# Node passes as later stages of the edge-attention loop, with one wait per chunk on GpSimd's gathers

## The chip, the cores and the metric

The kernel runs on one core of one Trainium2 chip. The metric is the device time of one execution in microseconds (us). Before the change it is 2722.23 us, the median of 3 runs (2716.83 to 2722.79).

## The reference, cut to what matters

A graph of 6250 nodes (128 features) and 100000 edges, sorted by their target `dst`. First comes a graph transformer layer, then a message layer; each is added to its input and normalised.

```python
q, k, v = x @ Wq, x @ Wk, x @ Wv                        # 8 heads of 16
scores = einsum('ehd,ehd->eh', q[dst], k[src]) / sqrt(16)
ex = exp(scores - segment_max(scores, dst)[dst])
alpha = ex / (segment_sum(ex, dst)[dst] + 1e-9)
agg = segment_sum(alpha[:, :, None] * v[src], dst)
h1 = layer_norm(x + agg @ W0, ln1_g, ln1_b)
ff = relu(h1 @ fc1_w + fc1_b) @ fc2_w + fc2_b           # 512 hidden
x1 = _layernorm(x + layer_norm(h1 + ff, ln2_g, ln2_b))
# message layer: for each half of the edges, over [x1[src], edge_attr, req]
m = relu(cat @ W1 + b1) @ W2 + b2
h = (1 + eps) * x1 + segment_sum(m_forward, dst) + segment_sum(m_backward, dst)
out = _layernorm(x1 + relu(h @ Wu + bu))
```

## The kernel before, in words

**Stages.** A start forms the table `kvq_tab` (keys, values, queries of all nodes) and the tables of chunks. Then come an edge loop, the node passes, and a message loop.

**Edge loop.** The edges are cut into 56 chunks of 1792 (128 lanes of 14), each with a window of 128 nodes. GpSimd gathers keys and values of a chunk with 14 indirect DMAs (L670, `gather_chunk`) into one of RING = 4 slots; a chunk has four pieces of 4, 3, 4 and 3 gathers (PIECES). A chunk passes through stages on the other engines: `passes4` runs one body for the chunk `new`, with `a_`, `b_`, `c_`, `e_` the chunks one to four before it.

- `new`: TensorE spreads the window's queries over the edges with one-hot matrices (L1078, `queries`, one PSUM bank a piece; it posts `l_q`). VectorE multiplies them by the keys and sums per head (L1445, L1447, `scores`), then takes running maxima (L1456, L1457; it posts `l_ml`).
- `a_`: two transposes (L1092, L1093, post `l_lr`), scans across the lanes (L1463 to L1465, `across`), two transposes back (L1112, L1113, post `l_cd`).
- `b_`: VectorE forms the differences to the maximum (L1472 to L1477), ScalarE the exponentials (L848 to L850), VectorE one-hot masks (L1494) and the weighted values (L1499, two halves, post `l_pva` and `l_pvb`). TensorE sums them over the window in 14 products (L1102, posts `l_agg`).
- `c_`: ScalarE copies the sums (L839), VectorE divides and adds what is carried between windows (L1485 to L1490, `averages`), TensorE transposes (L1118) and carries (L1119, post `l_ra`).
- `e_`: ScalarE copies the transposed averages into `nodes`, which holds all nodes (L843).

ScalarE also forms the one-hot matrices of a chunk two ahead (L811, L815, L816, `lane_masks`), from two lines of lane positions that VectorE subtracts (L1436, L1437, `lanes`) and ScalarE scales (L809).

What sets the order is the code itself: each engine has its body with waits in it, and nothing is reordered. A gather's slot is free when `l_pvb` of four chunks before is posted; beyond that, piece 1 of a chunk waits for `l_agg`, piece 2 for `l_q` and piece 3 for `l_lr`, all posted by TensorE.

**Node passes** (`passes3`, ten groups of five tiles of 125 nodes): W0, first normalisation, fc1, relu, fc2, second and third normalisation, the product `y` with the upper part of W1, stored to `y_tab`. ScalarE takes square roots (L871), normalises (L880) and copies; GpSimd adds and multiplies rows (L693 to L704), and clears the accumulators of the message loop (L700, L701).

**Message loop.** It gathers rows of `y_tab` (L727), adds the edge attributes (TensorE L1239, VectorE L1635), applies relu (ScalarE L957), sums over the window (L1252), accumulates (L1626, L1628), and normalises and stores a finished window. ScalarE's L976 and L979, and VectorE's L1649, stand in that last part. The gathers wait for the products of four chunks before (`m_agg`), a post of TensorE.

## Time and profile before

| | before |
|---|---|
| time, median of 3 runs | 2722.23 us |
| the profiled execution | 2717.23 us |
| its span, first to last instruction | 2715.2 us |
| busy: TensorE (PE) | 1557.6 us, 57% |
| TensorE weight loads (PEld) | 1227.2 us, 45% |
| VectorE (DVE) | 1442.3 us, 53% |
| ScalarE (ACT) | 748.1 us, 28% |
| GpSimd (POOL) | 1592.9 us, 59% |
| mean granted TensorE clock | 0.719 |
| moved by DMA | 251.96 MB, 93 GB/s |

Busy time counts neither waits nor the issuing of a DMA that goes through a queue; GpSimd's indirect gathers are instructions of their own and do count. A share is an average over stages with different limits. In the chain that ended last, 29% of the span is "issue", time in which the engine waited for nothing that the profile shows, 25% TensorE, 19% "another core or an unknown queue" (in rows: "remote"), 15% VectorE.

### The profile page before, as it was taken

How to read it: one execution, taken by the hardware profiler on the slowest of the kernel's cores; microseconds unless marked ns; L12 is line 12 of the kernel's file. 1: busy time of each engine (PE TensorE's matmuls, PEld its weight loads, DVE VectorE, ACT ScalarE, POOL GpSimd, SP SyncE). 2: the span in 40 equal slices, each digit the busy share in tenths (PEclk: the TensorE clock that was granted, in tenths of full speed). 3: DMA queues.
4: the chain of work that ended last, by engine and by line, in shares of the span. 5: the costliest groups of instructions: out<-in, count | busy, mean ns of one | idle time of the engine just before them, and what ended most of it. 6: DMA issues, size and time to landing. Idle time of an engine off the chain costs nothing.

```text
span 2715.2 us, 32144 instructions
## 1 busy us (share of the span) xinstructions
PE 1557.6 (57%) x7355; PEld 1227.2 (45%) x7356; DVE 1442.3 (53%) x2972; ACT 748.1 (28%) x1512; POOL 1592.9 (59%) x1662
## 2 busy tenths in 40 slices
PE   6354565556555555556786354556465565654656
PEld 4244455545545554455664233344343443433434
DVE  5265666666666666666575134345254353443535
ACT  3333333333433333333574011111111111111111
POOL 3665666666666666662532756665656656656661
PEclk9567767767777676767898566677677776767767
DMA  7554444444444444442011211221211212211221
GB/s 250 146 172 140 141 135 133 132 145 133 133 129 146 133 133 129 146 133 76 18 42 44 54 47 51 51 57 49 54 50 50 58 51 52 55 51 50 54 54 28
DMA packets 148256, 251.96 MB, mean 93 GB/s; under 512 B 74681, under 2 KB 99401, under 8 KB 147179
## 3 DMA queue, kind: packets, MB, share of 16 engines
q0 software_dynamic: 64048, 156.29, 20.2%
q1 hardware_dynamic: 83612, 94.45, 11.3%
q10 hardware_dynamic: 560, 0.82, 0.1%
q8 instruction: 13, 0.21, 0.0%
q14 instruction: 23, 0.19, 0.0%
HBM read 229.88 MB, written 21.54 MB: 93 GB/s over the span
## 4 chain that ended last, share of the span: by engine, by line
issue 29%; PE 25%; another core or an unknown queue 19%; DVE 15%; DVEq 5%; ACT 3%; DMA 2%; POOL 0%; SPq 0%; ACTq 0%; PEldq 0%; POOLq 0%
PE ps L1102 10%; PE ps L1078 8%; DVE arena L1626 4%; DVE arena L1635 2%; DVEq L1655 2%; DVE arena L1499 1%; ACT arena L880 1%; DVEq L1654 1%; PE ps L1029 1%; DMA arena<-d 1%; PE ps L1119 1%; DVEq L1652 1%; DVE arena L1445 1%; DVE arena L1554 1%
## 5 line engine op out<-in xcount | busy, mean ns | idle before, releaser
L670 POOL DMA_INDIRECT arena<-kvq_tab,arena x784 | 748.1, 954 | 455.7 <-issue 249.2
L727 POOL DMA_INDIRECT arena<-y_tab,arena x784 | 742.6, 947 | 447.5 <-issue 229.1
L1252 PEld LDWEIGHTS ps<-arena 128*128 128x128 f32 x1568 | 294.5, 255 | 407.5 <-issue 376.6
L1252 PE MATMUL ps<-arena 128*128 128x128 f32 x1568 | 319.1, 346 | 268.4 <-issue 250.9
L1102 PE MATMUL ps<-arena 128*128 128x136 f32 x1568 | 322.0, 393 | 245.7 <-issue 132.3
L1102 PEld LDWEIGHTS ps<-arena 128*128 128x128 f32 x1568 | 312.4, 297 | 268.2 <-issue 268.2
L957 ACT ACTIVATE arena<-arena 128x512 f32<-128x512 f32 x224 | 119.4, 569 | 800.1 <-DVE arena L1635 504.8
L1078 PE MATMUL ps<-arena 128*128 128x128 f32 x1596 | 286.7, 350 | 72.1 <-issue 32.3
L1239 PE MATMUL ps<-w1blk,eaT 113*128 x456 | 284.9, 709 | 64.8 <-issue 64.2
L1078 PEld LDWEIGHTS ps<-arena 128*128 128x128 f32 x1596 | 265.9, 258 | 98.4 <-issue 98.4
L1445 DVE TENSOR_TENSOR arena<-ps,arena 128x512 f32<-128x512 f32 x224 | 136.9, 611 | 320.8 <-remote 316.0
L1635 DVE TENSOR_TENSOR arena<-ps,arena 128x512 f32<-128x512 f32 x224 | 128.4, 618 | 318.0 <-remote 256.2
L816 ACT ACTIVATE arena<-arena 128x1792 f32<-128x1792 f32 x58 | 189.7, 3271 | 0.0
L1628 DVE TENSOR_REDUCE arena<-arena 128x128 f32<-128x1792 f32 x57 | 182.2, 3196 | 2.0
L1447 DVE TENSOR_REDUCE arena<-arena 128x32 f32<-128x512 f32 x224 | 139.2, 622 | 7.7
L1239 PEld LDWEIGHTS ps<-w1blk,eaT 113*128 113x128 f32 x456 | 95.2, 252 | 80.0 <-issue 80.0
L1494 DVE TENSOR_TENSOR arena<-ps,arena 128x1792 f32<-128x1792 f32 x56 | 113.3, 2024 | 26.9 <-issue 14.7
L1649 DVE BATCH_NORM_STATS2 arena<-ps 128x6 f32<-128x128 f32 x56 | 16.4, 292 | 202.2 <-remote 155.2
L826 ACT ACTIVATE arena<-arena 128x15 f32<-128x15 f32 x57 | 12.4, 217 | 384.5 <-issue 282.1
L1499 DVE TENSOR_TENSOR arena<-arena,ps 128x896 f32<-128x896 f32 x112 | 116.2, 1079 | 0.0
L1626 DVE TENSOR_TENSOR arena<-ps,arena 128x1792 f32<-128x1792 f32 x57 | 114.3, 2005 | 0.0
L1661 DVE TENSOR_TENSOR arena<-arena,ps 128x128 f32 x56 | 16.2, 289 | 171.9 <-issue 140.6
(258 smaller groups left out, 1973.1 us busy)
## 6 DMA issues: line engine op xcount, KB each, us to landing
arena<-d SPq DMA_DIRECT2D x59, 897.0 KB
arena<-kvq_tab,arena POOLq DMA_INDIRECT x784
arena<-y_tab,arena POOLq DMA_INDIRECT x784
kvq_tab<-arena SPq DMA_DIRECT2D x7, 1344.0 KB, 7.0
arena<-in_edge_attr_dram SPq DMA_DIRECT2D x60, 112.0 KB
y_tab<-arena SPq DMA_DIRECT2D x10, 625.0 KB
arena<-kvq_tab SPq DMA_DIRECT2D x59, 64.0 KB
out_dram<-arena SPq DMA_DIRECT2D x56, 64.0 KB
```

What stands on the lines that cost most here:

```text
L670: g.indirect_dma_start(kv_s[:, r, t, :], None, kvq_tab.rearrange("n (a d) -> (n a) d", a=3), bass.IndirectOffsetOnAxis(ap=v3(idx, RING)[:, ...
L727: g.indirect_dma_start(yg_s[:, r, t, :], None, y_tab, bass.IndirectOffsetOnAxis(ap=v3(idx1, RING)[:, r, t:t + 1], axis=0)).then_inc(m_g[r] ...
L816: a.activation(hotT.rearrange("n (u g e) -> n u g e", u=2, g=G)[:, u, :, :], line.rearrange("n (e g) -> n g e", g=G), ACT.Relu, scale=-1.0 ...
L1078: last = mm(bank(k)[:, t * D:(t + 1) * D], hotT_s[:, u, s0 + t, :], v3(qwin, 2)[:, u, :])
L1102: last = mm(sums, hot_s[:, u, t, :], contrib_s[:, u, t * RW:(t + 1) * RW], start=(t == 0), stop=(t == G - 1))
L1239: mm(bank(j)[:, 0:n * D], eaT_s[:, u, k * P:(k + 1) * P], w1blk[:, ds(way + a0 * D, n * D)]).then_inc(m_u, 1)
L1252: last = mm(bank(6 + u)[:, 0:W], yg_s[:, r, t, :], hot1_s[:, u, t, :], start=(t == 0), stop=(t == G - 1))
L1445: tt(keys, v3(bank(k)[:, 0:n * D], n), keys, ALU.mult).then_inc(l_prod, 1)
L1499: tt(contrib_s[:, u, s0:s1, :, 0:DH], kv_s[:, r, s0:s1, D:2 * D].rearrange("p g (h w) -> p g h w", h=H), weights.rearrange("p (g h) -> p g ...
L1626: link(tt(hot1_s[:, u, :, :], columns1[:, None, :].to_broadcast([P, G, W]), dcr1[:, :, None].to_broadcast([P, G, W]), ALU.is_equal))
L1628: v.tensor_reduce(v3(hsum, 2)[:, u, :], hot1_s[:, u, :, :].rearrange("p g n -> p n g"), AX_X, ALU.add).then_inc(m_hot, 1)
L1635: tt(rows_, v3(bank(j)[:, 0:n * D], n), rows_, ALU.add).then_inc(m_hid, 1)
```

## The change

The node passes go as a stage of their own. Their work is done for each chunk's window of 128 nodes, as four later stages of the edge loop (`passes8`, with LEAD = 8 passes ahead of the loop and 8 behind it):

- `e_`: ScalarE copies the transposed averages to `aggT` instead of `nodes`; TensorE multiplies by W0 and adds the window's features with a placement matrix (`sh`, `xw`), which SyncE loads from x and from the new table `moves` (`load_features`).
- `f_`: moments and first normalisation.
- `g_`: transpose, fc1, relu, fc2, and with them the scaled transpose and the features again for the sum.
- `h_`: moments, second normalisation with the sum, moments, third.
- `k_`: transpose, copy into `nodes`, `y`, and SyncE's store to `y_tab` (`store_y`).

The root's inverse is now `Exp(-0.5 * Ln(v + eps))` on ScalarE (`unit`) in place of a square root and a reciprocal. `lanes` goes from VectorE; two small products on TensorE from `dd` (two activations) give the same lines. The queries use two PSUM banks, not four: pieces 2 and 3 of a chunk are computed in its own pass, pieces 0 and 1 of the next chunk at the end of the pass. GpSimd keeps the waits for the index load and for `l_pvb`. Clearing the accumulators moves to VectorE, ahead of the message loop. SyncE's first loads for the message loop move into the passes that empty the pipeline.

The core of the diff:

```diff
-ITERS0 = -(-(NB0 + N // W - RING) // RING)
+LEAD = 2 * RING
+ITERS0 = -(-(NB0 + N // W - LEAD) // RING)
+        def passes8(eng, one_pass, n):
+            for c in range(LEAD):
+                one_pass(c % RING, *(c - k if c >= k else None for k in range(9)))
+            with eng.Fori(0, n) as i:
+                for c in range(RING):
+                    one_pass(c, *(i * RING + (c + LEAD - k) for k in range(9)))
+            for c in range(8):
+                one_pass(c % RING, *(n * RING + (c + LEAD - k) if k > c else None for k in range(9)))
...
+            def load_features(chunk, r):
+                base = entry0(chunk, 2, N - W)
+                sp.dma_start(v3(xw, RING)[:, r, :], x[ds(base, W), :]).then_inc(l_xw[r], 16)
+                lower = entry0(chunk, 3, W)
+                sp.dma_start(v3(sh, RING)[:, r, :], moves[ds(lower, P), :]).then_inc(l_xw[r], 16)
...
             def gather_chunk(r):
                 pool.wait_ge(l_ix[r], landed)
                 pool.wait_ge(l_pvb, slot_free)
                 for k, (s0, n) in enumerate(PIECES):
-                    if k:
-                        pool.wait_ge(s_init, 3)
-                    if k == 1:
-                        pool.wait_ge(l_agg, slot_free)
-                    if k == 2:
-                        pool.wait_ge(l_q, asked)
-                    if k == 3:
-                        pool.wait_ge(l_lr, turned_)
...
+            def unit(at):
+                link(a.activation(lnv[at], mv[at][:, 1:2], ACT.Ln, bias=eps_ln[:, :]))
+                return a.activation(rstd[at], lnv[at], ACT.Exp, scale=-0.5)
+            def normalised(to, rows_, at):
+                link(unit(at))
+                link(a.activation(shift[at], neg[at], ACT.Identity, scale=rstd[at]))
+                return a.activation(to, rows_, ACT.Identity, scale=rstd[at], bias=shift[at])
...
+                if h_ is not None:
+                    act.wait_ge(n_v2, minus7)
+                    unit(1).then_inc(n_s2, 1)
...
+                if g_ is not None:
+                    act.wait_ge(n_fcp, minus6)
+                    for c in range(FC):
+                        last = a.activation(v3(ffT, FC)[:, c, :], bank(2)[:, c * W:(c + 1) * W], ACT.Relu, bias=fc1b_all[:, c:c + 1])
+                    last.then_inc(n_f1s, 1)
...
+                if g_ is not None:
+                    pe.wait_ge(n_n1, minus6)
+                    last = tp(bank(3)[:, 0:W], h1n, ident[:, :])
+                if k_ is not None:
+                    pe.wait_ge(n_x1, minus8)
+                    last = tp(bank(3)[:, W:2 * W], x1, ident[:, :])
+                if new is not None:
+                    queries(u, 2, True)
+                if e_ is not None:
+                    pe.wait_ge(l_avT, minus4)
+                    mm(seven[:, W:2 * W], aggT, w0_sb[:, :], start=True, stop=False)
+                    last = mm(seven[:, W:2 * W], v3(sh, RING)[:, r, :], v3(xw, RING)[:, r, :], start=False, stop=True)
...
+                    pe.wait_ge(n_f1s, minus6)
+                    for c in range(FC):
+                        mm(six[:, 2 * W:3 * W], v3(ffT, FC)[:, c, :], fc2_sb[:, c, :], start=(c == 0), stop=False)
+                    last = mm(six[:, 2 * W:3 * W], h1Tr, ident[:, :], start=False, stop=True)
+                if a_ is not None or c_ is not None or g_ is not None:
+                    last.then_inc(l_cd, 1)
...
                 if new is not None:
                     scores(r, 0)
                 if b_ is not None:
                     differences((r + 2) % RING)
+                if f_ is not None:
+                    dve.wait_ge(n_res, minus1)
+                    link(moments(0, v3(res, 2)[:, 1 - u, :]))
+                    ts(neg[0], mv[0][:, 0:1], -1.0, None, ALU.mult).then_inc(n_v1, 1)
                 if new is not None:
                     scores(r, 1)
+                if h_ is not None:
+                    dve.wait_ge(l_cd, minus2)
+                    moments(1, bank(6)[:, 2 * W:3 * W]).then_inc(n_v2, 1)
+                    stt(tq, bank(6)[:, 2 * W:3 * W], mv[1][:, 0:1], g2_rows[:, :], ALU.subtract, ALU.mult).then_inc(n_tq, 1)
+                if new is not None:
+                    steps(1 - u, (r + 1) % RING)
                 if b_ is not None:
                     masks(u)
                     weighted(u, (r + 2) % RING)
+                if h_ is not None:
+                    stt(s3, tq, rstd[1], bank(6)[:, 3 * W:4 * W], ALU.mult, ALU.add).then_inc(n_s3, 1)
+                    link(moments(2, s3))
```

**GpSimd in the edge loop.** The first block is one chunk before the change, and the second two chunks of the changed kernel (L682 is the gather, formerly L670).

```order
L670 DMA arena<-kvq_tab,arena 128x256 [waits l_pvb,l_ix0,s_init]
L670 DMA arena<-kvq_tab,arena 128x256 x3
L670 DMA arena<-kvq_tab,arena 128x256 [waits l_agg,s_init]
L670 DMA arena<-kvq_tab,arena 128x256 x2
L670 DMA arena<-kvq_tab,arena 128x256 [waits l_q,s_init]
L670 DMA arena<-kvq_tab,arena 128x256 x3
L670 DMA arena<-kvq_tab,arena 128x256 [waits l_lr,s_init]
L670 DMA arena<-kvq_tab,arena 128x256 x2
L672 ISA
```

```order
L682 DMA arena<-kvq_tab,arena 128x256 [waits l_pvb,l_ix0,s_init]
L682 DMA arena<-kvq_tab,arena 128x256 x13
L684 REGISTER_ALU
L682 DMA arena<-kvq_tab,arena 128x256 [waits l_pvb,l_ix1,s_init]
L682 DMA arena<-kvq_tab,arena 128x256 x13
L684 REGISTER_ALU
```

The three waits inside a chunk's gathers are gone, and the fourteen follow one another.

**ScalarE in a pass of the edge loop.** Before, this is the stretch from the copy of the sums to the lane lines. After, the stretch from the exponentials to the product `y`; L827 is the Ln and L828 the Exp of `unit`, L887 the copy of the embedding, L894 the relus, L899 the copy of `y`.

```order
L839 ACTIVATE arena<-ps 128x136 [waits l_agg]
L841 ISA
L841 TENSOR_LOAD tab_sb
L841 ISA x2
L843 ISA [waits l_ra]
L843 ACTIVATE nodes<-ps 128x128
L848 ACTIVATE ps<-arena 128x112 [waits l_d,l_lr]
L849 ACTIVATE arena<-arena 128x112
L850 ACTIVATE arena<-arena 1x8
L826 ACTIVATE arena<-arena 128x15 [waits l_dif]
L827 ACTIVATE arena<-arena 128x8x13
L829 REGISTER_ALU
```

```order
L878 ACTIVATE ps<-arena 128x112 [waits l_d,l_lr]
L879 ACTIVATE arena<-arena 128x112
L880 ACTIVATE arena<-arena 1x8
L827 ACT_TABLE_LOAD
L827 ACTIVATE xs<-xs,eps_ln 128x1 [waits n_v2]
L828 ACT_TABLE_LOAD
L828 ACTIVATE xs<-xs 128x1 [waits n_al]
L887 ACTIVATE xs<-ps 128x128 [waits n_emb]
L889 ACTIVATE arena<-ps 8x256
L894 ACTIVATE xs<-ps,fc1b_all 128x128 [waits n_fcp]
L894 ACTIVATE xs<-ps,fc1b_all 128x128 x3
L899 ACTIVATE xs<-ps 128x256 [waits n_yfree,n_yp]
```

The exponentials are now followed by a normalisation's Ln and Exp, each with a table load of its own; the same pair of loads comes before each of the other two normalisations of a pass, so six loads a chunk. The lane masks come later, after the copies of the embedding, the relus and the copy of `y`.

## Rows read from the trace of the kernel before

Engines in the rows: PE is TensorE, PEld its weight loads, DVE VectorE, ACT ScalarE, POOL GpSimd. A stretch's row has its start and end, its length, the busy us (and count of instructions) of PE, PEld, DVE, ACT and POOL, TensorE's granted clock, the share of the DMA engines' time and GB/s. A group's row has line, engine, operation, output and input and their shapes and the count, then busy us and mean ns of one, then the idle us just before them and what ended most of it. A timeline's row has start and length in us, and in brackets the idle time before it and what ended that.

**Rows 1.** Busy time of each engine in the three stages.

```profile
67.00:1244.00 1177.00, 650.67 (x3390) 583.67 (x3391) 742.07 (x1613) 414.67 (x705) 747.85 (x784) 0.70 0.46 139
...
1295.00:1491.00 196.00, 148.50 (x852) 116.54 (x852) 125.17 (x442) 118.12 (x222) 75.33 (x42) 0.90 0.10 34
1491.00:2715.00 1224.00, 682.97 (x2758) 470.84 (x2758) 506.61 (x731) 174.75 (x509) 742.72 (x785) 0.69 0.20 51
```

**Rows 2.** Groups by line, whole span.

```profile
L670 POOL DMA_INDIRECT arena<-kvq_tab,arena x784 | 748.1, 954 | 455.7 <-issue 249.2 <-remote 188.4 <-PE ps L1078 15.7
...
L1445 DVE TENSOR_TENSOR arena<-ps,arena 128x512 f32<-128x512 f32 x224 | 136.9, 611 | 320.8 <-remote 316.0 <-PE ps L1078 4.9
...
L839 ACT ACTIVATE arena<-ps 128x136 f32<-128x136 f32 x56 | 15.9, 284 | 188.3 <-remote 171.7 <-PE ps L1102 16.6
```

**Rows 3.** Timeline of POOL in the edge loop.

```profile
703.93 0.96 POOL L670 DMA_INDIRECT arena<-kvq_tab,arena  x1 [0.30 <-issue]
708.46 0.95 POOL L670 DMA_INDIRECT arena<-kvq_tab,arena  x1 [3.57 <-remote]
...
729.40 0.94 POOL L670 DMA_INDIRECT arena<-kvq_tab,arena  x1 [2.93 <-remote]
```

**Rows 4.** Timeline of PE in the edge loop.

```profile
728.52 2.92 PE L1078 MATMUL ps<-arena 128*128 128x128 f32 x12 [0.36 <-issue]
...
745.84 0.27 PE L1118 MATMUL ps<-ident,arena 128*128 128x128 f32 x1 [2.23 <-issue]
748.66 0.39 PE L1119 MATMUL ps<-arena 128*1 128x136 f32 x1 [2.56 <-issue]
```

**Rows 5.** Timeline of ACT in the edge loop.

```profile
749.57 0.29 ACT L839 ACTIVATE arena<-ps 128x136 f32<-128x136 f32 x1 [3.92 <-remote]
```

**Rows 6.** Timeline of DVE in the edge loop.

```profile
728.81 0.69 DVE L1445 TENSOR_TENSOR arena<-ps,arena 128x512 f32<-128x512 f32 x1 [6.14 <-remote]
...
734.81 2.08 DVE L1499 TENSOR_TENSOR arena<-arena,ps 128x896 f32<-128x896 f32 x2
```

**Rows 7.** Message loop: one stretch of its start, and timelines of DVE and POOL.

```profile
1531.00:1557.00 26.00, 4.84 (x9) 2.59 (x9) 0.56 (x1) 0.81 (x3) 19.73 (x21) 0.50 0.20 53
...
1557.96 0.69 DVE L1635 TENSOR_TENSOR arena<-ps,arena 128x512 f32<-128x512 f32 x1 [26.04 <-remote]
...
1559.96 0.94 POOL L727 DMA_INDIRECT arena<-y_tab,arena  x1 [0.30 <-issue]
...
2030.56 0.69 DVE L1635 TENSOR_TENSOR arena<-ps,arena 128x512 f32<-128x512 f32 x1 [3.68 <-remote]
```

**Rows 8.** Timeline of ACT after the last gather, and in the node passes.

```profile
1235.32 0.36 ACT L848 ACTIVATE ps<-arena 128x112 f32<-128x112 f32 x1 [3.05 <-PE ps L1093]
...
1249.82 0.36 ACT L848 ACTIVATE ps<-arena 128x112 f32<-128x112 f32 x1 [0.55 <-DVE arena L1477]
...
1288.63 0.20 ACT L864 ACTIVATE mark<-eps_ln 128x1 f32<-128x1 f32 x1
...
1296.06 1.28 ACT L871 ACT_TABLE_LOAD   x1
1297.36 0.30 ACT L871 ACTIVATE arena<-arena,eps_ln 128x5 f32<-128x5 f32 x1
```

**Rows 9.** One stretch of the edge loop, and groups by line.

```profile
800.00:1000.00 200.00, 114.41 (x611) 103.59 (x611) 130.05 (x288) 73.64 (x125) 127.93 (x134) 0.72 0.43 134
...
L880 ACT ACTIVATE arena<-arena 128x128 f32<-128x128 f32 x100 | 40.7, 484 | 9.3 <-DVE arena L1561 9.3
...
L976 ACT ACTIVATE arena<-ps,bucol 128x128 f32<-128x128 f32 x56 | 20.0, 358 | 4.8 <-PE ps L1273 4.8
...
L1649 DVE BATCH_NORM_STATS2 arena<-ps 128x6 f32<-128x128 f32 x56 | 16.4, 292 | 202.2 <-remote 155.2 <-issue 44.2 <-PE ps L1273 2.8
...
L979 ACT ACTIVATE arena<-arena,eps_ln 128x1 f32<-128x1 f32 x56 | 16.3, 290 | 2.6 <-DVE arena L1650 2.6
...
L700 POOL MEMSET arena<- 128x12756 f32 x1 | 10.7, 10731 | 0.0
```

More of the change, by code:

```diff
@@ L110, in gnn_kernel @@
         i1 = dram("i1", (ALL1,), I32)
+        moves = dram("moves", (2 * P, W), F32)
         tab1 = dram("tab1", (TE, TF), I32)
@@ new lines, in sp_edges @@
+            def sp_edges(r, new, a_, b_, c_, e_, f_, g_, h_, k_):
+                u = r % 2
+                if new is not None:
+                    if b_ is not None:
+                        sp.wait_ge(s_d0, 48)
+                        sp.wait_ge(l_dcr, picked)
+                    load_heads(new + 2, (r + 2) % RING)
+                    sp.wait_ge(s_arr, 16 * 3)
+                    sp.wait_ge(l_q, asked)
+                    load_queries(new + 2, u)
+                    sp.wait_ge(s_d0, 48)
+                    sp.wait_ge(l_hT, formed)
+                    load_line(new + 3)
+                    sp.wait_ge(s_arr, 16 * 3)
+                    sp.wait_ge(l_ml, ended)
+                    load_index(new + 4, r)
+                if new is None and a_ is not None:
+                    sp.wait_ge(s_tabi, 48)
+                    for c in range(RING):
+                        load_chunk(c, c)
+                if b_ is not None:
+                    sp.wait_ge(s_tab0, 3)
+                    sp.wait_ge(s_move, 32)
+                    if g_ is not None:
+                        sp.wait_ge(l_cd, seen)
+                    load_features(b_, (r + 2) % RING)
+                if k_ is not None:
+                    store_y(k_, u)
+                for c in (ended, picked, formed, seen, turned8):
@@ L1031, in _ @@
                     turn_table()
+            pe.wait_ge(s_tab0, 2)
+            for f in range(2):
+                last = tp(bank(7)[0:1, (f + 1) * TE:(f + 2) * TE], tbe[0:TE, f + 2:f + 3], ident[0:TE, 0:TE])
+            last.then_inc(s_turn, 1)
             pe.wait_ge(s_ca, acts(PT - 1))
@@ L1083, in queries, with pe_edges @@
                         pe.reg_add(window, window, 16)
-            def pe_edges(r, new, a_, b_, c_, e_):
+            def pe_edges(r, new, a_, b_, c_, e_, f_, g_, h_, k_):
                 u = r % 2
                 w = 1 - u
-                left_right, sums, carried, turned = bank(4), bank(5)[:, 0:RW], bank(6), bank(7)
+                left_right, sums, six, seven = bank(4), bank(5)[:, 0:RW], bank(6), bank(7)
+                if type(new) is int and new == 4:
+                    pe.wait_ge(s_wn, 16 * 9)
+                    pe.wait_ge(s_tab0, 3)
+                    for c in range(FC):
+                        last = mm(bank(2)[:, c:c + 1], fc1_sb[:, c * P:(c + 1) * P], ln1_cols[:, 1:2])
+                    last.then_inc(n_b1, 1)
+                if type(new) is int and new == 6:
+                    pe.wait_ge(n_fc1, 2)
+                    pe.wait_ge(n_b1s, FC)
+                if type(new) is int and new == 7:
+                    pe.wait_ge(s_w4, 16 * LATE)
                 if a_ is not None:
@@ L1120, in pe_edges @@
-                if new is not None:
-                    queries(w, 2, True)
-                    queries(w, 3, True)
-                for c in (minus1, minus2, minus3, minus4):
+                for c in (now, minus1, minus2, minus3, minus4, minus6, minus7, minus8, minus9):
                     pe.reg_add(c, c, 1)
-            for k in range(NP_):
+            for k in range(2):
                 queries(0, k, False)
-            passes4(pe, pe_edges, n0, 4)
+            passes8(pe, pe_edges, n0)
@@ L1196, in turn_rows @@
-            def turn_rows(new, old, out_):
-                if out_ is not None:
-                    pe.wait_ge(n_ys, out_ + 2)
-                if new is not None:
-                    pe.wait_ge(n_res, new + 1)
-                pe.wait_ge(n_x1, old + 1)
-                transposes(bank(0, 2), res2, n_xTp)
-            for c in range(FC):
-                last = mm(bank(4)[:, c:c + 1], fc1_sb[:, c * P:(c + 1) * P], ln1_cols[:, 1:2])
-            last.then_inc(n_b1, 1)
-            pe.sem_inc(n_xTp, 1)
@@ L1519, in dve_edges @@
                     averages(1 - u, (r + 1) % RING, c_)
-                if new is not None:
-                    steps(1 - u, (r + 1) % RING)
-                    lanes((r + 2) % RING)
                 if new is not None:
```

625 lines of the change are left out of this document (260 added, 365 removed).

## The prediction

> **What bounds the kernel now.** I read the table of stretches first, to see which stages the time is in. The three rows [rows 1] are the first edge loop, the node passes and the message loop. Both loops issue 784 gathers on GpSimd (POOL); 1177 us / 56 chunks = 21.0 us a chunk in the first. The node passes are 196 us in which TensorE works 148.5 and GpSimd 75.3, and no gather runs.
>
> Next, who sets those 21 us. The groups by line [rows 2] say that a gather takes 954 ns, and that VectorE and ScalarE lose most of their idle time to "remote": 316 us before the score products L1445, 172 us before the copy L839. The timeline of GpSimd [rows 3] shows the rhythm: a gather each 0.95 + 0.30 = 1.255 us, 14 in a row 17.3 us with one short stop, and once a chunk a gap of 3.57 or 2.93 us ended by "remote". What stands still outside that gap is TensorE. Its two last transposes and carry products start at 745.84 and 748.66, 2.2 and 2.6 us apart with no producer named [rows 4], although the gathers run without a break there. The copy L839, which needs nothing but the 14 aggregation products, starts at 749.57 after 3.92 us of "remote" [rows 5], and L1445 of the chunk before, with its queries long computed, starts at 728.81 after 6.14 us [rows 6], 0.6 us before the gap at 729.40 ends. I read this as: **while GpSimd issues gathers without a break, TensorE's completions (and much of its issue) hardly get through; they come in a burst 2 to 3 us after the last gather.** (The gap of 2.93 less those 0.6 is 2.3, the gap of 3.57 less 0.6 is 3.0 [rows 3]; I take 2.8.) VectorE then needs 728.81 to 736.8 = 8.0 us to the end of the weighted values L1499 [rows 6].
>
> The message loop tests that reading. At its start 56 gathers run unpaused; in 26 us of them TensorE starts 9 matmuls, VectorE one instruction, and VectorE waits 26.04 us in one piece [rows 7]. Against it: a product at 2030.56 came through in the middle of a run after 3.68 us [rows 7]. So the hold leaks somewhat.
>
> Without gathers ScalarE's L848 goes from 1235.32 to 1249.82 [rows 8]: a pass costs 14.5 us, so the gathers cost 6.4 us of each chunk.
>
> **What the change does to GpSimd.** Now a slot's fourteen gathers wait for their index load and for `l_pvb` of four chunks before, and nothing else. Before, pieces 1, 2 and 3 also waited for `l_agg`, `l_q` and `l_lr`, all posted by TensorE, so that GpSimd could not run far ahead of it. With the ring of four full, the next gathers start when VectorE posts L1499 of a chunk and run 14 x 1.255 = 17.6 us to the start of the next, 17.3 to the end of the last. Everything VectorE then needs from TensorE (queries of pieces 2 and 3, `l_cd`) is posted after those weighted values are read, so inside the hold. The cycle closes on itself: 0.5 us to resume + 17.3 of gathers + 2.8 to the burst + the chain to the next L1499. That chain was 8.0 us [rows 6] with the queries of the whole chunk ready. Now there stand in it the moments of the embedding (three instructions) and those of the feed-forward with a scaling (three), each about 0.3 by the nearest row, L1649's 292 ns [rows 9], so 1.9 us, and the steps, 0.2; with one more link between engines I take 10.3. **T = 0.5 + 17.3 + 2.8 + 10.3 = 30.9 us a chunk, against 21.0.** Bounds of T: 25, if as much leaks as at 2030.56 and the burst comes before the gathers end; 34, if pieces 2 and 3 of the scores, whose queries are now only half a chunk ahead, fall into the next burst.
>
> **What it does to ScalarE.** It has 73.64 us of work in 200 [rows 9], 7.7 a chunk. It gains, per chunk: six table loads (each Ln and each Exp of the three normalisations has its own), at 1.28 each [rows 8] 7.7; ten instructions on one column or one number at L979's 0.29, 2.9; two normalisations and the scaled copy at L880's 0.484, 1.45; eight copies and relus of 128x128 at L976's 0.358 and the wider y copy at 0.484 [rows 9], 3.35. Together 15.4, so 23.1 us a chunk, packed. That is below T = 30.9: covered. It is above today's 21.0, so without the hold ScalarE would be the bound.
> The row shows the table load's 1.28 us and the next instruction at 1297.36, 0.02 us after it [rows 8]. The Trainium skill ("ScalarE: Activation LUTs", What ACT_TABLE_LOAD costs) adds a drain and comes to 2.66 us a switch; by that ScalarE would be at 23.1 + 6 x 1.38 = 31.4 us a chunk, just above T. The row shows no such drain, and it decides. The same page (Table sets: the hidden batching unit) has one set with both Ln and Exp, which would need one load for all; the build has six, so I count six.
>
> **TensorE, VectorE, SyncE.** TensorE goes from 36 to 52 matrix products a chunk; let go, it runs 12 instructions in 2.92 us [rows 4], so the some 20 products between burst and weighted values, two instructions each, take about 10: its own time just hides behind VectorE's chain of 10.3, if no answer of ScalarE's stands between; if one does, that is the upper end. VectorE loses the two lane instructions and gains about 3.5 us, of which 2.1 lie in the chain. SyncE adds a load of 128 KB and a store of 128 KB a chunk, and past them only its next loads are queued, two passes ahead: nothing; the DMA engines are busy 0.46 of the first loop [rows 1]. The clearing of the accumulators, 10.7 us and more on GpSimd [rows 9], moves to VectorE at the start of the message loop, where it waits for 26 us at one place [rows 7]: hidden; if not, +11 and somewhat more.
>
> **Sum.** Before, the message loop starts at 1491. After: the first 56 gathers run unpaused from 67 to 138, the burst is at 141, and the first weighted values, behind two passes and a half of scores, at 160. Fifty-one more at 30.9, less 7 for the first ones, whose passes lack the node stages: 1729. Gathers and burst once more: 1750, L1499 of the 53rd chunk 1760. Then no gathers are left and ScalarE's packed work sets the pace: 25 us to the next L1499, 15 to the end of the last full pass, and eight passes that empty the pipeline, an estimated 17.9 for the first two, which form no new lane masks, down to 4 for the last, together 108: 1908, and 5 to the last store and barrier: 1913. That is **+422**. Put the other way: before, the edge loop and its tail end at 1289 [rows 8] and 202 us of node passes and barriers follow; these go, and the loop with its tail grows by 624. The message loop keeps its waits: 1224. The profiled execution took 2717.2 (span 2715.2), 5.0 under the median 2722.2, within what its runs differ. 2717.2 + 422 = 3139; I say 3140. Each us of T is 51 us of time, and T = 30.9 - 422 / 51 = 22.6 would break even.
>
> **Rivals.**
> *Partial leak* (T 25 to 28): for it the product at 2030.56. At T = 26, 3140 - 51 x 4.9 = 2890. 0.16.
> *A longer chain* (T over 34, or ScalarE's loads dearer): pieces 2 and 3 in the next burst, or Ln waiting on VectorE and back within the burst. At T = 34, 3300; with the skill's drain T = 33, about 3250. The part over 3310 has 0.06.
> *The other side: TensorE's completions are not held on this path, and ScalarE is the bound.* Then the waits taken out cost nothing, the node passes vanish under the loop, and the time is decided by ScalarE's packing: from the 141 of the start, 141 + 56 x 23.1 = 1435 against 1491, so -56: 2661. It wins up to (1491 - 141) / 56 = 24.1 us a chunk; with 1.7 us of waits a chunk between its own links it would be at 2756. For it: the 196 us that go are real, and the gap that ends a hold may be a wait for the very semaphores that are removed, so that the pause was the cause of nothing. Against it: the message loop, where 26 us pass with no such wait. 0.12.
> *The change doesn't do what it says*: the table loads could be skipped when executed; ScalarE is then at 15.4 a chunk, and under the hold nothing changes: 3140 still.
>
> **How the numbers follow.** The hold with T from 28 to 34: 0.63, its own range 2990 to 3300. Leak 0.16, longer or dearer 0.06, ScalarE-bound and faster 0.12, about equal 0.03. 0.2% (5 us) is what a measurement of this kernel can tell from none. Faster 0.12, same 0.03, slower 0.85. The range leaves out those two and the part over 3310: 2780 to 3310.
>
> **What would show it.** Right: gathers of the first loop in blocks of 14 with one gap of 11 to 16 us, none inside; VectorE's and ScalarE's "remote" waits above 12 us a chunk; the first loop 1.4 times as long; TensorE's clock lower there. ScalarE busy near 23 us a chunk with six loads of 1.28, and not waited for. Wrong: gaps on GpSimd under 7 us, or ScalarE busy over 90% of a pass; then the hold was not there and the loads set the time. If L1499 comes much over 11 us after the burst, the chain term was too small.

## The result, and the profile after

| | before | after |
|---|---|---|
| time, median | 2719.53 us (4 runs, 2716.22 to 2722.79) | 3085.15 us (4 runs, 3078.35 to 3091.03) |
| ratio to before | | 1.134, 95% interval 1.131 to 1.137 |
| span of the profiled execution | 2715.2 us | 3082.6 us |
| busy: TensorE | 1557.6 us | 1594.0 us |
| VectorE | 1442.3 us | 1419.3 us |
| ScalarE | 748.1 us | 1360.3 us |
| GpSimd | 1592.9 us | 1514.5 us |

The change makes the kernel 13% slower; forecast were 3140 us, 2780 to 3310. A run over 1.5% longer than the fastest of the same kernel is slow and is compared with nothing; that was one run, in experiment 5. Busy time hardly grows except on ScalarE, and ScalarE is busy only 44% of the span. The stages show where the time went; these are stretches of the changed kernel, with the columns of [rows 1]:

```profile
67.00:1719.00 1652.00, 783.26 (x5017) 659.89 (x5017) 802.18 (x1975) 1036.62 (x2052) 743.85 (x784) 0.76 0.34 105
1719.00:1860.00 141.00, 85.19 (x440) 69.00 (x441) 62.20 (x179) 126.78 (x261) 0.00 (x0) 0.71 0.11 34
1860.00:3083.00 1223.00, 678.48 (x2758) 470.08 (x2757) 521.32 (x732) 175.09 (x508) 742.68 (x785) 0.70 0.20 51
...
600.00:1000.00 400.00, 197.36 (x1287) 165.82 (x1287) 203.44 (x509) 269.71 (x539) 172.59 (x182) 0.78 0.33 101
```

The edge loop up to its last gather takes 1652 us where it took 1177, the emptying of the pipeline 141 where tail and node passes took 247 (1244 to 1491), and the message loop 1223 where it took 1224: +475, -106, -1. In the 400 us from 600 on ScalarE is busy 269.7, two thirds, and each other engine about half of the time or less. Nothing is full, so the loop is bound by waits.

The groups by line of the changed kernel (L682 is the gather, L1422 the score products, L869 the copy of the transposed rows, the first in ScalarE's pass that needs a later product than the aggregation and the transposed averages), as in [rows 2]:

```profile
L682 POOL DMA_INDIRECT arena<-kvq_tab,arena x784 | 743.8, 949 | 930.2 <-DVE arena L1476 674.3 <-issue 255.9
...
L1422 DVE TENSOR_TENSOR arena<-ps,arena 128x512 f32<-128x512 f32 x224 | 138.7, 619 | 789.0 <-remote 764.8 <-issue 13.8 <-PE ps L1081 10.4
...
L869 ACT ACTIVATE xs<-ps 128x128 f32<-128x128 f32 x56 | 15.5, 277 | 369.3 <-remote 367.4 <-PE ps L1115 1.5 <-issue 0.2
```

GpSimd waits 674 us for VectorE's L1476, the weighted values (L1499 before); VectorE waits 765 us for "remote" before L1422, and ScalarE 367 before L869. That is a circle. The timelines show one turn of it; first GpSimd, against [rows 3]:

```profile
912.40 0.95 POOL L682 DMA_INDIRECT arena<-kvq_tab,arena  x1 [13.49 <-DVE arena L1476]
...
928.70 0.95 POOL L682 DMA_INDIRECT arena<-kvq_tab,arena  x1 [0.30 <-issue]
943.10 0.95 POOL L682 DMA_INDIRECT arena<-kvq_tab,arena  x1 [13.46 <-DVE arena L1476]
```

Fourteen gathers run from 912.40 to 929.65, then nothing for 13.46 us. The turns are 30.7 us long. TensorE and VectorE in the same turn:

```profile
910.75 3.48 PE L1153 MATMUL ps<-arena 128*128 128x136 f32 x28 [1.95 <-DVE arena L1476]
...
915.66 0.33 PE L1170 MATMUL ps<-identw,arena 128*128 128x128 f32 x1
...
916.56 1.16 PE L1176 MATMUL ps<-fc_sb,xs 128*128 128x128 f32 x8
...
917.78 1.73 PE L1081 MATMUL ps<-arena 128*128 128x128 f32 x14
...
924.22 0.47 PE L1115 MATMUL ps<-identw,xs 128*128 128x128 f32 x1 [4.39 <-ACT xs L834]
...
901.87 0.69 DVE L1422 TENSOR_TENSOR arena<-ps,arena 128x512 f32<-128x512 f32 x1 [14.34 <-remote]
...
909.53 2.08 DVE L1476 TENSOR_TENSOR arena<-arena,ps 128x896 f32<-128x896 f32 x2
...
932.57 0.69 DVE L1422 TENSOR_TENSOR arena<-ps,arena 128x512 f32<-128x512 f32 x1 [14.31 <-remote]
```

TensorE has finished the aggregation at 914.2, the transposed averages (L1170) at 916.0, fc2 (L1176) and, by 919.5, the queries (L1081) that VectorE's next L1422 needs; its records there are dense. VectorE starts it at 932.57, 13 us later and 2.9 us after the last gather has ended. Nothing but the report of that work (the semaphore post) is missing. The trace's semaphore events, which no view prints, have it directly: the posts for the second batch of products (carries and fc2, both pieces of the queries, the maxima's transposes, the transpose of 924.22) stand at 932.38 to 932.64, while those products end from 917.94 to 924.69. The other thing that L1422 needs, the landing of its gathers, stands at 888.12. ScalarE:

```profile
905.85 1.28 ACT L827 ACT_TABLE_LOAD   x1
907.25 0.29 ACT L827 ACTIVATE xs<-xs,eps_ln 128x1 f32<-128x1 f32 x1
...
924.57 0.26 ACT L851 ACTIVATE arena<-ps 128x136 f32<-128x136 f32 x1
924.73 0.27 ACT L854 ACTIVATE xs<-ps 128x128 f32<-128x128 f32 x1
...
932.66 0.28 ACT L869 ACTIVATE xs<-ps 128x128 f32<-128x128 f32 x1 [7.30 <-remote]
```

The two copies that need the aggregation (L851) and the transposed averages (L854) start at 924.57 and 924.73, without a wait, as soon as ScalarE comes to them: what TensorE finished up to 916.0, 3.6 us into the run of gathers, had been reported (the post for L1170 stands at 916.70). What it finished later had not: L869, which needs the transpose of 924.22, waits till 932.66 as VectorE does. Of the six loads of tables (1.28 us each, and their instruction 0.1 us behind) four lie in the stretch in which VectorE works, and two, at 920.21 and 921.81, ahead of the transpose of 924.22, whose report is held anyway. Whether they cost something is tested in experiment 2.

### The profile page after: what moved, and what is told of

Same layout as the page of the kernel before. It is cut to its first block, busy times and chain, and to the rows that moved or that the text cites. A ratio compares the mean times of both kernels' runs of the same rounds, so it can differ in the third digit from the quotient of the medians.

```text
span 3082.6 us, 37672 instructions
## 1 busy us (share of the span) xinstructions
PE 1594.0 (52%) x8385; PEld 1228.9 (40%) x8386; DVE 1419.3 (46%) x2981; ACT 1360.3 (44%) x2857; POOL 1514.5 (49%) x1622
## 3 DMA queue, kind: packets, MB, share of 16 engines
q1 hardware_dynamic: 105794, 99.14, 10.3%
## 4 chain that ended last, share of the span: by engine, by line
another core or an unknown queue 35%; issue 23%; DVE 22%; ACT 7%; PE 7%; DVEq 4%; DMA 1%; SPq 1%; ACTq 0%; POOLq 0%
DVE arena L1422 4%; DVE arena L1476 3%; DVE arena L1560 3%; PE ps L1218 2%; ACT L828 2%; PE ps L1231 2%; DVE arena L1569 2%; ACT L827 1%; DVEq L1589 1%; DVE arena L1471 1%; DVE xs L1481 1%; PE ps L1021 1%; DVEq L1588 1%; DVE arena L1424 1%
## 5 line engine op out<-in xcount | busy, mean ns | idle before, releaser
L682 POOL DMA_INDIRECT arena<-kvq_tab,arena x784 | 743.8, 949 | 930.2 <-DVE arena L1476 674.3
L711 POOL DMA_INDIRECT arena<-y_tab,xs x784 | 742.6, 947 | 573.4 <-issue 371.5
L1081 PE MATMUL ps<-arena 128*128 128x128 f32 x1582 | 268.4, 328 | 482.0 <-DVE arena L1422 423.6
L1422 DVE TENSOR_TENSOR arena<-ps,arena 128x512 f32<-128x512 f32 x224 | 138.7, 619 | 789.0 <-remote 764.8
L1231 PE MATMUL ps<-arena 128*128 128x128 f32 x1568 | 314.6, 343 | 282.9 <-issue 273.9
L1231 PEld LDWEIGHTS ps<-arena 128*128 128x128 f32 x1568 | 291.3, 253 | 415.3 <-issue 394.5
L1081 PEld LDWEIGHTS ps<-arena 128*128 128x128 f32 x1582 | 243.5, 237 | 499.1 <-issue 498.9
L1153 PE MATMUL ps<-arena 128*128 128x136 f32 x1568 | 205.6, 291 | 96.9 <-DVE arena L1476 96.9
L1153 PEld LDWEIGHTS ps<-arena 128*128 128x128 f32 x1568 | 196.1, 199 | 117.7 <-issue 117.6
L828 ACT ACT_TABLE_LOAD x168 | 215.5, 1283 | 3.0
L827 ACT ACT_TABLE_LOAD x168 | 215.5, 1283 | 3.0
L869 ACT ACTIVATE xs<-ps 128x128 f32<-128x128 f32 x56 | 15.5, 277 | 369.3 <-remote 367.4
L1115 PE MATMUL ps<-identw,xs 128*128 128x128 f32 x56 | 26.3, 470 | 242.1 <-ACT xs L834 220.2
L944 ACT ACTIVATE eaT<-ps 112x256 f32<-112x256 f32 x59 | 21.7, 367 | 258.9 <-remote 238.1
L1471 DVE TENSOR_TENSOR arena<-ps,arena 128x1792 f32<-128x1792 f32 x56 | 113.0, 2018 | 14.7 <-ACT arena L880 14.7
```

The costliest lines, as they stand in the source:

```text
L682: g.indirect_dma_start(kv_s[:, r, t, :], None, kvq_tab.rearrange("n (a d) -> (n a) d", a=3), bass.IndirectOffsetOnAxis(ap=v3(idx, RING)[:, ...
L711: g.indirect_dma_start(yg_s[:, r, t, :], None, y_tab, bass.IndirectOffsetOnAxis(ap=v3(idx1, RING)[:, r, t:t + 1], axis=0)).then_inc(m_g[r] ...
L827: link(a.activation(lnv[at], mv[at][:, 1:2], ACT.Ln, bias=eps_ln[:, :]))
L828: return a.activation(rstd[at], lnv[at], ACT.Exp, scale=-0.5)
L1081: last = mm(bank(k % 2)[:, t * D:(t + 1) * D], hotT_s[:, u, s0 + t, :], v3(qwin, 2)[:, u, :])
L1153: last = mm(sums, hot_s[:, u, t, :], contrib_s[:, u, t * RW:(t + 1) * RW], start=(t == 0), stop=(t == G - 1))
```

## The experiments

**Theory (hold):** while GpSimd issues gathers without a break, TensorE's completions stay back; the three waits of before made the breaks. **Rivals:** ScalarE's table loads made it slow; or the longer chain of stages did, whatever GpSimd does. All ratios below are to runs of the kernel before on the same chip, which took 2715.64 to 2729.84 us (medians). All of the chunk times are from the gathers of chunks 15 to 45 of each trace's edge loop, from the first of one to the first of the other, divided by 30; by this measure before has 20.9 us and the change 30.3.

### 1. The three waits back in the changed kernel

```diff
                 for k, (s0, n) in enumerate(PIECES):
+                    if k == 1:
+                        pool.wait_ge(s_init, 3)
+                        pool.wait_ge(l_agg, slot_free)
+                    if k == 2:
+                        pool.wait_ge(s_init, 3)
+                        pool.wait_ge(l_q, asked)
+                    if k == 3:
+                        pool.wait_ge(s_init, 3)
+                        pool.wait_ge(l_lr, turned_)
```

`asked` starts at BASE - 2 and grows by 4 a chunk: the first half of the queries of the chunk after `new`. `turned_` starts at BASE - 1 and grows by 1. The lines that make and raise these counters are left out, here and below. `s_init` is complete before the loop (its last post stands at 69.85 us in the changed kernel) and holds nothing up.

> The changed kernel with the three waits of before put back inside a chunk's gathers: piece 1 for the aggregation four chunks back, piece 2 for the queries of the next chunk's first half, piece 3 for the transposes of the pass after. Hold theory (TensorE's completions stay back while gathers run on, and come 2.8 us after the last): the pause lets them out once in the middle, so a chunk falls from 30.7 us to what ScalarE's 23.1 us of work plus some waits allow, 24 to 25; 3085 - 51 x 6.2 = about 2770 (2720 to 2850). Rival (the pauses are without effect, and the chain through four stages more is simply longer): 3085 or, with the pauses' 3 us a chunk on top, up to 3230.

Measured: 2738.1 us (2722.7 to 2750.4, 10 runs), ratio 1.002 (0.9995 to 1.005). 23.6 us a chunk. With the waits the whole loss of 13% is gone: with all four new stages, six table loads a chunk and the queries half a chunk ahead, it is even with before. One stretch, and GpSimd's gaps:

```profile
600.00:1000.00 400.00, 268.60 (x1639) 230.89 (x1639) 262.15 (x646) 346.55 (x699) 226.77 (x238) 0.79 0.42 132
...
814.10 0.95 POOL L693 DMA_INDIRECT arena<-kvq_tab,arena  x1 [3.23 <-DVE arena L1489]
...
820.68 0.95 POOL L693 DMA_INDIRECT arena<-kvq_tab,arena  x1 [1.87 <-remote]
...
836.20 0.96 POOL L693 DMA_INDIRECT arena<-kvq_tab,arena  x1 [3.27 <-DVE arena L1489]
```

Several shorter gaps (1.9 to 3.3 us here, up to 7.0 elsewhere in the loop), mostly after 4, 7 or 10 gathers, take the place of one of 13.5. ScalarE is busy 346.6 of 400; experiment 3 tests whether it is now the bound.

### 2. One table load in place of six a chunk

```diff
+            a.add_instruction(mybir.InstLoadActFuncSet(name=nc.get_next_instruction_name(), act_func_set_id=6,
+                engine=mybir.EngineType.Activation, ins=[], outs=[]))
             penalties(0, 0)
```

The loop uses Ln, Exp, Identity, Copy, Relu and Square; with set 6 loaded by hand ahead of it, the trace has no other table load between 70 and 1959 us.

> The changed kernel with one table set that holds Ln and Exp loaded once, so without the six table loads a chunk (7.7 us of ScalarE). Hold theory: ScalarE is not what a chunk waits for (30.7 us are gathers, burst and VectorE's chain), so the edge loop keeps 30.6 to 30.7 us a chunk; only the tail after the last gather, eight passes at ScalarE's pace, gets shorter by up to 8 x 5 = 40 us: 3045 to 3085. Rival (ScalarE's loads are what made the change slow): 56 x 7.7 = 430 less, about 2655.

Measured: 3062.8 us (3053.8 to 3068.6), ratio 1.121 (1.119 to 1.124). ScalarE's busy time and the tail, from the last gather (start at 1731.6) to the message loop's first (1836.2):

```profile
600.00:1000.00 400.00, 197.46 (x1271) 170.24 (x1272) 202.13 (x503) 167.20 (x459) 172.57 (x182) 0.74 0.33 101
...
1732.00:1836.00 104.00, 72.34 (x440) 61.57 (x441) 61.98 (x179) 62.08 (x211) 0.56 (x1) 0.83 0.16 48
```

ScalarE falls from 269.7 to 167.2 us of 400, from 20.4 to 12.8 us a chunk, and the chunk has 30.6 us where it had 30.3. The tail is 104.6 us in place of 143.2 (starts at 1716.9 and 1860.1); of these 38.6 us the loop, 15 us longer, takes some back. The medians differ by 22 us; by the ratios to before (1.134 and 1.121, on two chips) it is 35. The loads were covered in the loop. The rival of the loads falls.

### 3. Both together

> Both edits: the three waits and one table load. Hold theory: with the pause and without the loads ScalarE has 15.4 us a chunk, the gathers with one gap (17.3 + 3.5) bound again: 21 us a chunk, 3085 - 51 x 9.7 - 40 in the tail = about 2550 (2530 to 2620), faster than before, since the 196 us of node passes are really gone. Rival (loads alone): 2655 as with one load only. Rival (longer chain alone): 3045 to 3085.

Measured: 2758.6 us (2752.7 to 2767.2), ratio 1.011 (1.008 to 1.014), 25.0 us a chunk: a miss by 200 us, and slower than with the loads. The gaps are irregular, and what ends them is another:

```profile
802.17 0.95 POOL L693 DMA_INDIRECT arena<-kvq_tab,arena  x1 [4.83 <-PE ps L1167]
...
809.98 0.95 POOL L693 DMA_INDIRECT arena<-kvq_tab,arena  x1 [4.34 <-PE ps L1095]
812.03 0.95 POOL L693 DMA_INDIRECT arena<-kvq_tab,arena  x1 [1.11 <-issue]
...
827.42 0.95 POOL L693 DMA_INDIRECT arena<-kvq_tab,arena  x1 [3.14 <-remote]
...
L693 POOL DMA_INDIRECT arena<-kvq_tab,arena x784 | 746.4, 952 | 650.2 <-issue 258.3 <-PE ps L1167 206.6 <-PE ps L1095 156.1
```

Four gaps in 30 us, of 1.1 to 4.8 us, and a run of ten gathers between the last two. GpSimd waits 206.6 us in all for L1167, the aggregation, and 156.1 for L1095, the queries, with TensorE named: there TensorE's work itself was late, not only its report. The products of L1167 show it:

```profile
790.98 3.01 PE L1167 MATMUL ps<-arena 128*128 128x136 f32 x16 [3.08 <-DVE arena L1490]
...
798.47 0.39 PE L1167 MATMUL ps<-arena 128*128 128x136 f32 x1 [1.74 <-issue]
799.20 2.20 PE L1167 MATMUL ps<-arena 128*128 128x136 f32 x9 [0.35 <-issue]
```

The gathers of that stretch run to 797.34. Under them TensorE starts single products 0.9 to 1.7 us apart, and the last nine follow in a row 1.9 us after the gathers' end. Over the loop these 28 products take 10.0 us in the median chunk; in the changed kernel and in experiment 1 it is 3.5. So gathers hold back TensorE's issue too when they fall on such work. ScalarE was not what bound experiment 1, since its busy time fell without any gain. Why the kernel without the loads comes to lie so badly is not shown; 7 and 8 show which wait mends it.

### 4. The kernel before without its three waits

```diff
-                    if k:
-                        pool.wait_ge(s_init, 3)
-                    if k == 1:
-                        pool.wait_ge(l_agg, slot_free)
-                    if k == 2:
-                        pool.wait_ge(l_q, asked)
-                    if k == 3:
-                        pool.wait_ge(l_lr, turned_)
```

> The kernel before with the three waits inside a chunk's gathers taken out, nothing else: one wait per chunk as in the change. Hold theory: 0.5 + 17.3 + 2.8 + 8.0 = 28.6 us a chunk in place of 20.9: +7.7 x 51 = +390, about 3110 (3000 to 3150). Rival (the waits are a cost or nothing): 2719 or less.

Measured: 3072.1 us (3065.6 to 3078.8), ratio 1.125 (1.123 to 1.128), 27.5 us a chunk. No stage moved, no table load, no longer chain: taking out the three waits alone costs nearly as much as the whole change (1.134). GpSimd's first gather of two chunks (L662), and VectorE's score products, differences and weighted values (L1437, L1464, L1491):

```profile
811.36 0.95 POOL L662 DMA_INDIRECT arena<-kvq_tab,arena  x1 [0.30 <-issue]
822.63 0.95 POOL L662 DMA_INDIRECT arena<-kvq_tab,arena  x1 [10.32 <-DVE arena L1491]
...
850.24 0.95 POOL L662 DMA_INDIRECT arena<-kvq_tab,arena  x1 [10.33 <-DVE arena L1491]
...
810.82 0.69 DVE L1437 TENSOR_TENSOR arena<-ps,arena 128x512 f32<-128x512 f32 x1 [10.23 <-remote]
...
815.05 0.23 DVE L1464 SCALAR_TENSOR_TENSOR arena<-ps,arena 128x8 f32<-128x8 f32 x1 [2.82 <-remote]
...
819.73 2.08 DVE L1491 TENSOR_TENSOR arena<-arena,ps 128x896 f32<-128x896 f32 x2
```

The gathers end at 812.3 and VectorE's queries were reported 1.5 us before that, at 810.8; but the carries for L1464 only at 815.05, 2.7 us behind. The 1.1 us that are missing to the expected 28.6 are such a leak. The rival of the longer chain falls too.

### 5. A stop on GpSimd that waits for nobody

```diff
                 for k, (s0, n) in enumerate(PIECES):
+                    if k == 2:
+                        pool.wait_ge(m_gap, gap_)
+                        pool.reg_add(gap_, gap_, 1)
+                        g.tensor_tensor(idle_.rearrange("p (b c) -> p b c", b=11), ones[:, None, :].to_broadcast([P, 11, P]),
+                                        ones[:, None, :].to_broadcast([P, 11, P]), ALU.add).then_inc(m_gap, 1)
```

`idle_` is an unused tile of 128x1408 and `ones` the constant, repeated; `m_gap` is posted by the addition itself, one chunk before.

> The changed kernel, no wait on another engine added: after seven of a chunk's fourteen gathers GpSimd does one addition of 128x1408 constants into an unused tile, some 3.4 us by the 1.55 us of a 128x640 one in the kernel before. Hold theory (what keeps TensorE's completions back is the unbroken issue of gathers): the stop is long enough for the burst, 2.8 us after the seventh, VectorE's chain of 10 us runs under the second seven, and a chunk falls from 30.7 to 23.5 to 26 us: 2720 to 2850. Rival (only waiting for TensorE helps, because it orders the two engines): nothing gained, 3.4 us a chunk more, 3085 to 3280.

Measured: 2813.8 us, one run (the other took 2889.0), 1.035 of before; 25.0 us a chunk. One run gives no interval, but it is 271 us less than the change, and even the other is 196 less, far outside of what runs of one kernel differ by here. GpSimd, and VectorE's L1430 (the score products):

```profile
825.19 0.95 POOL L690 DMA_INDIRECT arena<-kvq_tab,arena  x1 [0.30 <-issue]
826.16 2.54 POOL L687 TENSOR_TENSOR xs<-ones 128x1408 f32<-128x1408 f32 x1
828.86 0.95 POOL L690 DMA_INDIRECT arena<-kvq_tab,arena  x1 [0.16 <-issue]
...
828.17 0.69 DVE L1430 TENSOR_TENSOR arena<-ps,arena 128x512 f32<-128x512 f32 x1 [4.22 <-remote]
```

The seventh gather ends at 826.14, GpSimd adds for 2.54 us, and 2.0 us into this VectorE's wait ends, at 828.17. GpSimd was not idle and waited for nobody. The posts stand at 827.84 to 828.20 in the semaphore events. What lets the completions out is the break in the gathers.

### 6. One wait only

After seven gathers, for `l_q` and `asked` as in 1.

> The changed kernel with a single wait put back: after seven gathers, for the queries of the next chunk's first half. It lets out the carries, these queries and the transposes behind them. Hold theory: one burst in the middle and one before the run gives nearly what three waits gave: 2740 to 2800. If each of the three waits is needed, 2850 or more.

Measured: 2888.2 us (2883.2 to 2893.1), ratio 1.062 (1.056 to 1.069), 26.8 us a chunk. So one place gives 200 us of the 350, not nearly all; the expectation of 2740 to 2800 was wrong, and its other case came.

### 7. Which posts have to come out

A pass needs TensorE's posts in two batches: carries, transposes and the next chunk's first half of queries; then, after ScalarE's answer to the transposes, embedding, fc1, y and the second half. So: one wait for each. (A chunk's "own" queries are those of the chunk `new` in whose pass the gathers start; the gathers themselves fill the slot of the chunk two later.) `half_` starts at BASE - 4 and grows by 4 a chunk.

```diff
+                    if k == 0:
+                        pool.wait_ge(s_init, 3)
+                        pool.wait_ge(l_q, half_)
+                    if k == 2:
+                        pool.wait_ge(s_init, 3)
+                        pool.wait_ge(l_q, asked)
```

> One table load, and two waits on TensorE's queries: before the first gather for the second half of the chunk's own (the batch with embedding and fc1), after seven gathers for the next chunk's first half. Two gaps of 2.9 us a chunk with 17.6 of gathers are 23.4 us: 3063 - 51 x 7.3 = 2690 (2660 to 2760). With three waits and one load it was 24.6 a chunk, 2759. Rival (with ScalarE's loads gone the pauses come at random whatever the waits): 2750 or more.

> The same with the second wait after four gathers in place of seven. After four gathers completions still came through without a burst (the posts up to 4.3 us behind a run's first gather did), so the gap there is only as long as TensorE works, but it comes at 5 us where the queries are posted at 7 to 8: about the same, 2680 to 2760; later in the run ten gathers in a row hold longer. Rival: as before, 2750 or more.

Measured, both with one table load: 2630.8 us (two runs, 2629.5 and 2632.0), ratio 0.968 (0.963 to 0.972), with the second wait after seven gathers, 22.4 us a chunk, below the 2660 to 2760 expected; 2695.0 (2693.2 to 2707.2), ratio 0.993 (0.990 to 0.995), with it after four, 23.9 a chunk. The first is faster than before; the second is within 1% of it. The first timed again, and with the six loads kept:

> The same two waits with one table load, timed again over more rounds: 2631 (2622 to 2645), a ratio of 0.967 to before.

> The two waits on the queries' halves (before the first gather and after seven), with the six table loads a chunk kept. With them ScalarE has about 20.3 us of work a chunk by the changed kernel's trace (three waits: busy 346.6 of 400 at 23.5 us a chunk), and its links cost some us more, so it should bind at 23 to 24 us: 2630.8 + 51 x 1.5 = 2710 (2680 to 2745). If it comes to 2630 too, the loads are hidden under the gaps and only the place of the waits counts.

Measured: 2634.0 us (2629.3 to 2645.4), ratio 0.970 (0.967 to 0.972); with the loads 2669.3 (2663.9 to 2676.3), ratio 0.982 (0.979 to 0.985). The loads cost 35 us, and not in the loop (22.4 a chunk with them, 22.5 without) but in the tail, 134.8 us against 90.6; the loop, 9 us shorter with them, gives some back. The expectation that ScalarE binds with them was wrong. GpSimd's gaps in the first, and one stretch:

```profile
711.23 0.95 POOL L691 DMA_INDIRECT arena<-kvq_tab,arena  x1 [2.52 <-remote]
...
722.35 0.95 POOL L691 DMA_INDIRECT arena<-kvq_tab,arena  x1 [2.66 <-remote]
...
733.38 0.95 POOL L691 DMA_INDIRECT arena<-kvq_tab,arena  x1 [2.56 <-remote]
...
600.00:1000.00 400.00, 270.68 (x1711) 231.59 (x1710) 270.02 (x668) 226.92 (x619) 236.08 (x249) 0.84 0.45 138
```

In this stretch the gap is 2.5 to 2.7 us after each seven gathers, 11.0 to 11.1 us from one to the next. Of the 106 stops in the loop 78 follow seven gathers; six runs are of fourteen, with 3.7 to 9.2 us behind them.

### 8. Each wait's part

> One table load, and of the two waits only the one before a chunk's first gather (the second half of the chunk's own queries). Where a chunk's own half is late it makes one gap longer, but the fourteen gathers stay unbroken: near the kernel with one load and no wait, 3063 (3000 to 3130). If the place before the first gather were what helps, 2800 or less.

> One table load, the three waits of before, and the fourth before a chunk's first gather. Three waits and one load took 2759, the two waits on the queries' halves 2631. If what was missing there was the batch with embedding and fc1, this comes to 2630 to 2670. If the waits for aggregation and transposes themselves cost (they hold the gathers for work that is not needed yet), it stays near 2759.

Measured: 3047.0 us (3044.1 and 3050.0) with only the wait ahead of the first gather, ratio 1.122 (1.117 to 1.128): fourteen gathers in a row, 30.7 us a chunk, nothing gained. 2613.3 us (2610.8 and 2615.8) with all four waits, **ratio 0.963 (0.958 to 0.967)**, the shortest time here, by two runs; its interval touches that of the two waits (0.967 to 0.972). So the waits of 3 did not cost; what was missing there was the wait before the first gather, which does nothing alone. With it, three waits and one load are 145 us faster than without it (133 by the ratios), and the 28 products of the aggregation take 3.5 us again in the median chunk. The runs show this gain; that it comes from letting out the second batch is argued, not shown.

```profile
713.30 0.94 POOL L697 DMA_INDIRECT arena<-kvq_tab,arena  x1 [2.63 <-remote]
...
724.29 0.95 POOL L697 DMA_INDIRECT arena<-kvq_tab,arena  x1 [2.54 <-remote]
...
600.00:1000.00 400.00, 269.36 (x1746) 230.99 (x1746) 278.07 (x684) 231.10 (x634) 239.59 (x252) 0.87 0.46 140
```

## Why the prediction was right

**Right, point by point.** The circle was the one forecast, and its terms came near. A turn was taken as 0.5 to resume, 17.3 of gathers, 2.8 to the burst and 10.3 of chain, 30.9; the turn shown has 0.8 (911.61, the end of L1476, to 912.40), 17.25 (912.40 to 929.65), 2.9 (to 932.57) and 9.7 (901.87, the start of L1422, to 911.61): 30.7. No term is off by more than 0.6 us, and the differences nearly cancel. Experiments 1, 4 and 5 show the cause: waits back, loss gone; waits out of the kernel before, the same loss; a stop that waits for nobody, 271 of 365 us gone. That ScalarE's loads were covered in the loop is shown by 2, and the row with 1.28 us and no drain behind a load held: the 336 loads of the loop and its tail have a mean of 1283 ns, and without them ScalarE's busy time falls by 102.5 us of 400, 7.6 a chunk. By the 2.66 us a switch that the Trainium skill gives ("ScalarE: Activation LUTs", What ACT_TABLE_LOAD costs) it would be 16; the trace does not agree with that for these loads. The same page's set with both functions exists and does what it says (experiment 2), as soon as it is loaded by hand.

**Signs that did not come.** Two of the signs named for being right were missed. TensorE's granted clock was not lower in the loop but higher, 0.76 where it was 0.70. And only VectorE's "remote" waits are above 12 us a chunk (764.8 / 56 = 13.7); ScalarE's before L869 are 6.6 (367.4 / 56). Neither is part of the sum.

**The 55 us between 3140 and 3085.** Three terms of the sum.
- *"Fifty-one more at 30.9, less 7":* the changed kernel takes from 166.6 (the first gather that had to wait) to 1700.6, where the last block begins, 1534 us for 51 turns: 30.1. The usual turn is 30.7. The first five, up to 305, take 138 us, 15 less than five usual ones, where the forecast took off 7; and five later ones take 27.5 (see the last section). Together 1534 against 1569, -35; the start was 6 us later than 160.5.
- *The tail, "25 and 15" and "108":* forecast 166 us from the end of the last gather to the message loop, measured 142 (1717.9 to 1860.1), -24. ScalarE's work per pass was mis-sized: 23.1 us by the sum of single durations, 20.4 by the trace (269.7 / 400 x 30.3), since instructions that follow each other overlap: four relus take 1.09 us together and were counted at 1.43.
- *The message loop:* 1222.5 in place of 1224. The clearing was hidden, as forecast. It stands between 1867.60 and 1884.93 on VectorE, ahead of waits of 18 and 24 us:

```profile
1867.60 10.69 DVE L1611 MEMSET arena<- 128x12756 f32 x1 [2.60 <-PE ps L1218]
1879.56 5.37 DVE L1612 MEMSET arena<- 2x6378 f32 x1 [1.27 <-issue]
...
1911.24 0.56 DVE L1569 TENSOR_TENSOR arena<-ps,arena 128x384 f32<-128x384 f32 x1 [18.26 <-remote]
1935.78 0.69 DVE L1569 TENSOR_TENSOR arena<-ps,arena 128x512 f32<-128x512 f32 x1 [23.98 <-PE ps L1218]
```

**What was wrong in the reading.** "TensorE's completions (and much of its issue) hardly get through": in the changed kernel's turn above its issue isn't slowed, the records up to 919.5 are dense; in experiment 3 it is, so the bracket holds where gathers fall on a long row of products. "Everything VectorE then needs is posted inside the hold" is right for what the circle needs, but the hold does not begin with the run: what was finished in its first 3.6 us came through, and what ended from 5.5 us on (917.94) did not.

**The rivals.** The faster side (0.12) had the right size of the prize and the wrong condition: 2661 was what comes if completions aren't held and ScalarE is the bound. With the pauses placed the kernel takes 2613 to 2634, and 2669 with the six loads kept, but a chunk takes the same 22.4 us there with and without them, so ScalarE's packing is not what sets it and the nearness of 2661 is luck. On the dearer side the "T = 33" has no working: the prediction's own sum gives 31.4 for ScalarE. The node passes in the loop are worth it; the one wait per chunk is what made the change cost 13%.

## What to carry to other kernels

A wait that looks like a pure cost can be what gives other engines their turn: before taking waits off an engine that issues gathers, look at whether other engines' "remote" waits end just after its gaps. Then place one break for each batch of posts that a pass needs in sequence; here mostly every seven gathers, 2.5 us each, instead of one gap of 13.5. When work moves into a loop, a shared table set is worth little while something else binds, and 35 to 40 us in the part that empties the pipeline.

## What the runs showed of the hardware that was not expected

- After seven gathers VectorE's wait ended 2.0 us behind the last one's end (826.14 to 828.17, experiment 5), after fourteen 2.9 us. By the semaphore events the first post of the burst is 1.7 us (827.84) and 2.7 us (932.38) behind it, and the five posts of 932.38 to 932.64 stand within 0.3 us.
- There is no fixed moment from which posts stay back. In the turn shown, what ended at 916.0, 3.6 us into the run, was posted at 916.70, and what ended at 917.94 only at 932.38. In experiment 5 the transposed averages that ended 4.1 us into a run (821.74, the run from 817.69) came at 827.84, and in experiment 4 one post came out in the middle of a run, at 810.72, 15.7 us after its start (795.04).
- A compute instruction on GpSimd of 2.5 us lets the posts out as an idle gap does. Which part of the chip is shared by gathers and TensorE's posts, and whether it is the issue of the gathers or their data, stays open; no run here separates it.
- In every ninth chunk GpSimd itself stops for 1.1 us after the first gather. In the changed kernel the turns of 27.5 us from 305 on are just these (starts at 550.55, 823.45, 1096.47, 1369.67 and 1642.44). With one table load (experiment 2) such turns take 27.7 to 31.2 us, so what so short a stop lets out depends on where it falls.
